# Filling the half-swapped input tile by copies on the chip instead of a second load from DRAM

## The reference, cut to what matters

```python
x = x + _L0_conv_ref(_gn(x), dw, pw, att, glob)   # stage 0
x = x + _L1_conv_ref(_gn(x), w_off, w_conv, b)    # stage 1

# stage 0: a 3x3 depthwise convolution, then three 32x32 channel mixes (softmax, 1x1, softmax)
# stage 1, a deformable 3x3 convolution:
off  = conv3x3(x, w_off)                # 64 channels: a row and a column offset for each pixel
rows = clip(off_row + r, 0, H - 1); cols = clip(off_col + c, 0, W - 1)
mapped = bilinear sample of x at (rows, cols)      # floor, ceil, four values, two blends
out  = conv3x3(mapped, w_conv) + b
```

## Time and profile before

| | us |
|---|---|
| median of 3 runs | 717.24 |
| lowest and highest run | 716.29, 727.23 |
| the profiled execution: its time | 718.9 |
| the profiled execution: its span | 717.1 |

### The profile page before, as it was taken

The page is one execution under the profiler, slowest core; times in us unless marked ns, Lnnn a source line. Parts: engine busy times, 40 slices in busy tenths (PEclk is TensorE's granted clock), DMA queues, the critical chain, the costliest instruction groups (busy, mean ns, idle before and its releaser), DMA issues.

```text
span 717.1 us, 10746 instructions
## 1 busy us (share of the span) xinstructions
PE 684.6 (95%) x3500; PEld 244.4 (34%) x3500; DVE 522.7 (73%) x1033; ACT 467.9 (65%) x812; POOL 478.1 (67%) x414
## 2 busy tenths in 40 slices
PE   4799979999999799999999999999999999999985
PEld 4333333333333233333333333333333333333322
DVE  3687988779956568677876589657984685578882
ACT  7587776686667365677556755576656775577870
POOL 5004867888597656866867765887658668788770
PEclk9999999999999899999999999999999999999998
DMA  8958926889557998799949896598947625477556
GB/s 142 187 111 144 143 57 158 179 178 196 126 141 165 189 213 204 171 209 189 203 112 233 173 209 152 138 236 171 225 112 177 154 66 139 114 170 178 123 118 147
DMA packets 140189, 115.64 MB, mean 161 GB/s; under 512 B 15168, under 2 KB 114016, under 8 KB 140128
## 3 DMA queue, kind: packets, MB, share of 16 engines
q1 hardware_dynamic: 116096, 103.12, 68.6%
q10 hardware_dynamic: 24032, 11.78, 9.2%
HBM read 31.59 MB, written 16.78 MB: 67 GB/s over the span
## 4 chain that ended last, share of the span: by engine, by line
PE 55%; SPq 5%; DVE 5%; ACT 3%; POOL 3%; issue 2%; DMA 1%; DVEq 0%; POOLq 0%; ACTq 0%
PE off_ps L794 27%; PE c_ps L683 24%; PE c_ps L694 2%; PE c_ps L698 2%; SPq L476 2%; SPq L395 1%; DVE other_row L1436 1%; SPq L427 1%; ACT other_row L988 1%; DMA x1b<-x1a 1%; ACT off_abs L1001 1%; DVE x1a L1421 1%; POOL row_diff L1213 1%; ACT down_ps L999 1%; POOL row_diff L1215 1%
## 5 line engine op out<-in xcount | busy, mean ns | idle before, releaser
L1436 DVE COPY_PREDICATED other_row<-down_ps,row_diff 128x768 f32<-128x768 int32 x128 | 124.7, 1028 | 124.2 <-ACT down_ps L999 124.0
L794 PE MATMUL off_ps<-x1a,wo 128*64 128x512 f32 x768 | 179.4, 601 | 4.3 <-DMA x1b<-x1a 3.7
L794 PE MATMUL off_ps<-x1b,wo 128*64 128x512 f32 x768 | 176.4, 592 | 0.0
L683 PE MATMUL c_ps<-xb,w 128*64 128x512 f32 x336 | 149.6, 593 | 2.2 <-DVE x1a L1421 1.6
L683 PE MATMUL c_ps<-mapb,w 128*64 128x512 f32 x336 | 150.8, 594 | 0.5 <-ACT bias L977 0.3
L685 PE MATMUL c_ps<-xa,w 128*64 128x512 f32 x336 | 149.6, 593 | 0.0
L988 ACT ACTIVATE other_row<-row_diff 128x768 f32<-128x768 f32 x128 | 100.7, 835 | 66.4 <-POOL row_diff L1215 43.8
L1230 POOL TENSOR_TENSOR other_row<-other_row,x_strips 128x512 f32<-128x512 f32 x48 | 57.2, 1191 | 119.1 <-DVE other_row L1448 119.0
L685 PE MATMUL c_ps<-mapa,w 128*64 128x512 f32 x294 | 131.7, 594 | 0.0
L999 ACT ACTIVATE down_ps<-off_ps,bias_o 128x512 f32<-128x512 f32 x64 | 42.0, 656 | 106.8 <-PE off_ps L794 99.4
L1231 POOL TENSOR_TENSOR other_col<-other_col,other_row 128x512 f32<-128x512 f32 x64 | 86.3, 1349 | 31.3 <-DVE other_row L1448 31.3
(11 more groups left out here) (135 smaller groups left out, 978.5 us busy)
## 6 DMA issues: line engine op xcount, KB each, us to landing
mapa<-mapped SPq DMA_DIRECT2D x224, 65.0 KB, 2.0
x1b<-x1a SPq DMA_DIRECT2D x28, 520.0 KB, 6.5
mapb<-mapa SPq DMA_DIRECT2D x28, 520.0 KB, 7.6
out_dram<-x1a SPq DMA_DIRECT2D x49, 256.0 KB, 4.7
xb<-in_x_dram SPq DMA_DIRECT2D x48, 256.0 KB, 9.9
xa<-in_x_dram ACTq DMA_DIRECT2D x40, 256.0 KB, 8.7
x_strips<-x1a SPq DMA_DIRECT2D x112, 81.2 KB, 2.5
x_strips<-x1a SPq DMA_DIRECT2D x112, 65.0 KB, 2.5
```

What stands on the lines that cost most here:

```text
L683: nc.tensor.matmul(bank[0:64, :], weights[:, kx, :], rows_b[:, of, kx:kx + W], start=(kx == 0), stop=(kx == 2))
L794: last = nc.tensor.matmul(off_ps[k % 2][64 * t:64 * t + 64, CH * n:CH * n + CH], wo[wpar][:, kx, side:side + 2 * C], rows[:, b:b + 7:2, kx ...
L1436: last = dve.copy_predicated(other_row[n][:, :, KR // 2 * odd:KR // 2 * odd + KR // 2, :], bass.AP(tensor=rows.tensor, offset=rows.offset ...
```

## The change

From image 1 on, `xb` is no longer loaded from DRAM. Once a half of `xa` has landed, SP copies it within SBUF to `xb`, whole rows with their pad columns, by two transfers of 64 partitions (one for each swapped half). Each takes runs of 16 x 130 floats, which is 520 KB a transfer, the size of an `x1b` copy. Where eight transfers of 256 KB were issued there are now four of 520 KB. Each copy waits for its half of `xa`, a wait that SP did not have. For images 3 to 7 the two halves are also put at different places of SP's list: the first half where the load stood, the second half behind the first half of the strips of the next image. ACT's wait ahead of `pad_x` counts two transfers a half instead of four.

```diff
...
@@ -448,15 +448,14 @@
                     sp.wait_ge(sem_, value)
                     sp.sem_inc(sp_step, 1)
 
-            def load_xb(i, half, loaded):
-
-                rows = x[i].rearrange("c (b r) w -> c b r w", r=4)
-                to = xb_of(i)
+            def copy_xb(i, half, copied):
+
+                to, rows = xb_of(i), xa_of(i)
                 b, e = half * HB, half * HB + HB
-                for q in range(4):
-                    first = b + 1 if q < 2 else b
-                    sp.dma_start(to[Q * q:Q * q + Q, first:first + HB, 1:W + 1], rows[:, b:e, (q + 2) % 4, :])\
-                      .then_inc(loaded[half], DMA)
+                for first, p, p_from in ((b + 1, 0, 2 * Q), (b, 2 * Q, 0)):
+                    sp.dma_start(to[p:p + 2 * Q, first:first + HB, :].rearrange("p b w -> p (b w)"),
+                                 rows[p_from:p_from + 2 * Q, b:e, :].rearrange("p b w -> p (b w)"))\
+                      .then_inc(copied[half], DMA)
 
             def copy_x1b(par, half):
                 n = NR // 4 * WP
@@ -514,7 +513,8 @@
                              conv_b.rearrange("(c o) -> c o", o=1)).then_inc(b_load, DMA)
             sp.wait_ge(cleared, 1)
             for half in range(2):
-                load_xb(1, half, ahead_xb_loaded)
+                sp.wait_ge(ahead_loaded[half], LOADS * DMA)
+                copy_xb(1, half, ahead_xb_copied)
 
             for strip in range(4):
                 sp.wait_ge(x1_ready, min(2 * strip + 3, 8))
@@ -525,7 +525,8 @@
                     sp.wait_ge(conv1_done, 8)
                     load_x(sp, 2, half, xa_loaded)
                 for half in range(2):
-                    load_xb(2, half, xb_loaded)
+                    sp.wait_ge(xa_loaded[half], xa_count(2))
+                    copy_xb(2, half, xb_copied)
 
             for i in range(NB):
                 prev, nxt, after = i >= 1, i + 1 < NB, i + 2 < NB
@@ -553,10 +554,9 @@
                     sp.wait_ge(mapa_moved[1], A_MOVES * DMA * i)
                     copy_mapb(1)
                 if after and prev:
-                    for half in range(2):
-
-                        sp.wait_ge(conv1_done, 8 * (i + 1) + (5 if half == 0 else 8))
-                        load_xb(i + 2, half, xb_loaded)
+                    sp.wait_ge(conv1_done, 8 * (i + 1) + 5)
+                    sp.wait_ge(xa_loaded[0], xa_count(i + 2))
+                    copy_xb(i + 2, 0, xb_copied)
                 if not prev:
                     sp.wait_ge(mapped_ready, 4)
                     sp.wait_ge(s_setup["dve"], 6)
@@ -568,8 +568,13 @@
                     sp.wait_ge(off_done, NK * i + 4)
                     copy_x1b((i + 1) % 3, 0)
                     sp.wait_ge(mapped_ready, NK * i + 4)
-                    for half in range(2 if i >= 2 else 1):
-                        move_strips(sp, i + 1, half)
+                    move_strips(sp, i + 1, 0)
+                    if prev and after:
+                        sp.wait_ge(conv1_done, 8 * (i + 1) + 8)
+                        sp.wait_ge(xa_loaded[1], xa_count(i + 2))
+                        copy_xb(i + 2, 1, xb_copied)
+                    if i >= 2:
+                        move_strips(sp, i + 1, 1)
                 if not nxt:
                     if i >= 2:
                         sp.wait_ge(out_ready, 8 * (i - 1))
@@ -619,7 +624,8 @@
                     for half in range(2):
                         load_x(sp, b, half, xa_loaded)
                     for half in range(2):
-                        load_xb(b, half, xb_loaded)
+                        wait_apart(xa_loaded[half], xa_count(v))
+                        copy_xb(b, half, xb_copied)
                     wait_apart(x1_pads, v + 1)
                     for half in range(2):
                         copy_x1b(0, half)
@@ -883,9 +889,9 @@
                 else:
                     for half in range(2):
                         if isinstance(i, int) and i == 1:
-                            act.wait_ge(ahead_xb_loaded[half], LOADS * DMA)
+                            act.wait_ge(ahead_xb_copied[half], COPIES * DMA)
                         else:
-                            act.wait_ge(xb_loaded[half], LOADS * DMA * (i - 1))
+                            act.wait_ge(xb_copied[half], COPIES * DMA * (i - 1))
                 rows_a, rows_b, mean = xa_of(i), xb_of(i), mean_x[par]
                 fill(rows_a[:, :, 0:WP:WP - 1], mean[:, :])
                 fill(rows_b[:, :, 0:WP:WP - 1], mean[:, :])
```

More of the change, by code:

```diff
@@ L251, in deformable_preact_kernel @@
         ahead_loaded = [sem(f"x_ahead_loaded{n}") for n in range(2)]
-        ahead_xb_loaded = [sem(f"x_ahead_xb_loaded{n}") for n in range(2)]
+        ahead_xb_copied = [sem(f"x_ahead_xb_copied{n}") for n in range(2)]
         x1b_written = sem("x1b_written")
         xb_written = sem("xb_written")
-        xb_loaded = [sem(f"xb_loaded{n}") for n in range(2)]
+        xb_copied = [sem(f"xb_copied{n}") for n in range(2)]
         x1b_copied = [sem(f"x1b_copied{n}") for n in range(2)]
```

## The result

| | median us | range | runs |
|---|---|---|---|
| before | 722.24 | 716.29 to 728.07 | 4 |
| with the change | 732.88 | 731.24 to 736.20 | 4 |

The four runs of before fall into two groups near 717 and 728, and the ratio, 1.023 with a 95% interval of 1.017 to 1.029, is that of the runs with the change to the two runs near 717. The profiled execution of the change took 733.4 us with a span of 731.6, against 718.9 and 717.1. The forecast was 722.5, with a range up to 728.5. The sign was right and the size was not. The time lies between the forecast and the rival that was slower by over 2% (736).

The account below looks back on a forecast made before the run. PE was taken to bound the kernel, busy 370 of 370 us from 252 to 622. Terms -3.2 + 5.6 + 3.0 = +5.4 on 718.9 gave 724.3, less 1.7 for the median 722.6, stated as 722.5; range 711.5 to 728.5.

Parts of the forecast that it names:

- the rival that was slower by over 2%: Late `xa` loads hold SP in image 4 and one later image, two 8 us gaps with low clock: 736 us, chance 0.1.
- The start, images 1 and 2: Eight loads become four copies, twice; new waits for `xa` fall into SP's 16.6 us of room, so nothing was counted.
- The price of a pair to the issues right behind it: In SP's list, a copy pair costs 1.3 us by itself and the issues behind it 3.3 us more.
- Image 3, a gain of 3.2 us: SP gains 1.5 us during image 1, PE's `x1b` gap in image 2 shrinks from 3.7 to 2.2: gain 3.2 us.
- Image 4, filled in image 2, a cost of 8.6 us: SP waits 4.4 us for late `xa`, `mapb` comes late: a new 5.6 us gap plus 3.0 us of low clock.
- Images 5 to 7, counted at nothing: SP 4.6 us later against room of 4.7, so 0 to 2 us; counted 0, PE's image 3 loss being room.
- The sum: Whole kernel: -3.2 + 5.6 + 3.0 = +5.4 us, given chance 0.45 and its own range of 719 to 727 us.
- The rule on turns between queues: DMA engines serve queues round-robin by packets, so ACT's late `xa` load gets its turn; the forecast set 21.1 us against it.
- the 10 us of an even share of the bytes: Rival for image 4: ACT's `xa` load gets half of 209 GB/s, no wait for `xa`; 714.7 us, chance 0.2.
- The 21.1 us of before: Landing time of image 4's last `xa` load, issued at 254.8 before the change; carried over to predict landing at 272.

Follow-up runs that it names:

- the one with the small pair: Against the kernel with image 4 loaded, the copy pair between the strips moved one block of 16 for images 3, 5, 6 and 7; 719.33 us, ratio 1.0015.
- the kernel with image 4 loaded: Against the change, image 4 alone had both halves of `xb` loaded from DRAM at the old place; 727.94 us, ratio 1.012.
- the first edit: Against the change, only images 1 and 2 were copied, both halves of images 3 to 7 loaded at the old place; 718.27 us, ratio 0.9994.
- Without the late load: Against the change, `xa` of image 4 was loaded behind chunks 1 and 3 of image 2, like the other images; 731.87 us, ratio 1.019.
- the kernel with only loads from image 4 on: Against the change, only images 1, 2 and the first half of image 3 were copied, all else loaded at the old place; 725.43 us, ratio 1.010.
- the one with copied first halves: Against the change, from image 3 on only first halves of 3, 5, 6 and 7 were copied, other halves loaded, all at the old place; 716.24 us, ratio 0.9967.
- a later load: Against the kernel with only loads from image 4 on, ACT's second half of `xa` came one chunk later in images 3 to 5; 713.98 us, ratio 0.9949.
- loads at the new place: Against the change, from image 3 on both halves were loaded from DRAM, the second still between the strips; 721.76 us, ratio 1.0045.

## Why the prediction was wrong

- **The start, images 1 and 2: right.** Copied or loaded is the same (0.9994).
- **The price of a pair to the issues right behind it: right.** 1.3 us and 3.3 more were taken, 1.2 and 3.0 were measured. For image 2 the forecast's terms without the wait for `xa` are 14.6 + 1.3 + 13.9 + 11.3 = 41.1 us from `x1b` to the store, and the list took 41.0.
- **Image 3, a gain of 3.2 us: wrong, it cost 2.1** (1.6 at `x1b`, 0.5 at `mapb`). The forecast had the `x1b` pair leave at 169.1 and take 14.6 us with its strips. It left 2.4 us later, at 171.46 (PE was 1.7 us late from the start), and took 15.9 (to 187.37). The first copy pair does not explain that, as it had landed by 168.2; the cause stays open. Behind the second pair the strips after the store took 11.4 us (10.6 before) and the second `mapa` 12.2 (11.8 before), where I had let SP's gain of 1.5 us carry through. In the six kernels that copy only the first half of image 3, and in the one with the small pair, the gain is there: PE waits 1.0 to 1.8 us for `x1b` and is then 4.0 to 5.1 us ahead of before. So the bytes of the second pair are what took it.
- **Image 4, filled in image 2, a cost of 8.6 us: wrong, it was 0.4.** SP was near the forecast, with the second `mapb` issue at 332.06 where it had 329.2. PE was not: it wanted `mapb` at 338.6 where the forecast had 331.6, since it was 3.8 us late and not 3.2 early, and it came when `mapb` had nearly landed (338.9). The 4.4 us wait for the second half of `xa` was not there: the load had landed at 274.8 when SP came at 275.1. The 12.3 us wait for its first half, which the forecast overlooked, was there and was covered by SP's wait for the pads of `x1a`.
- **Images 5 to 7, counted at nothing: this is the step that failed.** It is 10.7 of the 14.9 us. All of it falls in PE's image 4, 1.9 us as a wait for ACT and 8.8 at the `mapb` pair that stands in SP's list behind the pairs for image 5, filled in image 3. The forecast set SP's lateness at 4.6 us against a room of 4.7. In the kernel with image 4 loaded, the `mapb` pair of image 4 went out 9.3 us later than before with PE 1.7 later. So SP was 7.6 us late against PE and not 4.6: 1.1 at the start of the list, 5.0 in it, 1.5 behind it. PE lost 7.0 us there. At a landing of 7.4 us it would have waited 2.3. The landing, for which the forecast had no term here, took 3.4 more beside ACT's load, and the clock, at half for 3.4 us, cost the other 1.3. In the change, where the clock was at half for 6.8 us, it cost 2.9. "What PE lost in image 3 is room for the next images" held for no image, as PE lost 0.4 us there.
- **The sum.** Forecast -3.2, +8.6 and 0, measured +2.1, +0.4 and +10.7, and 1.7 us at the start that the runs of the first edit show not to be the change's. That the sign came out right was luck: the term that made it was not there, and the loss came from the one counted at nothing.
- **The rival slower than 2%** came nearest in time (736). It had two gaps of 8 us with low clock, where the trace has 5.3 and 5.85, but put them down to a late `xa` that spreads. Without the late load the time is the same (1.019 against 1.023, with intervals that overlap), so that is not the cause.
- **The rule on turns between queues.** The last of ACT's loads of `xa` for image 4 landed like this (count, KB, us to landing):

```profile
xa<-in_x_dram ACTq DMA_DIRECT2D x1, 256.0 KB, 16.9
```

That is 18.3 us for the half from its first issue, at 256.44, not the 10 us of an even share of the bytes. The 21.1 us of before, which the forecast carried over, are no measure of long rows: what SP had on the engines from 253 to 256 was its load of `xb`, 1054 packets with 0.52 MB, so rows of 512 bytes. By the page "DMA: Bandwidth & Descriptors" of the Trainium skill, section "Queues, rings and completion order", the turns go by packets, and this trace does not contradict that: ACT's rows are of 512 bytes and a row of the copies is of 8,320. Equal turns can then be unequal bytes. No run here separates this from other reasons.

What stays open: why the copied pair in SP's list costs up to 2.7 us more than four loads of the same bytes at the same place (41.0 against 38.3 us in image 2), so that the bytes are not the whole price, and why the kernel with only loads from image 4 on has a longer list in image 3 than the one with copied first halves (37.9 against 36.7).

## What to carry to other kernels

Here a copy within SBUF in place of a load from DRAM relieved neither the DMA engines, which moved 115.87 MB instead of 115.64, nor the list behind it, in which the strips behind a copied pair took longer than behind the loads. Count a transfer by what it holds up behind it, and in every stage that it is placed in. When a queue is only a few us ahead of need, look up what another queue issues just behind that point: being late past it costs the collision as well as the delay, and in this kernel 2.6 us of lateness made 7 us between two traces (9 between the medians). Before giving up a change, move the thing that it collides with, since a later load turned 725 into 714 us.

## What the runs showed of the hardware that I had not expected

- Two 520 KB copies within SBUF land 7.1 to 7.6 us after the first issue with nothing near them. With 1 MB of loads from another queue issued at the same moment it is 10.4 to 11.9 us.
- An issuing engine can be held up by the transfers of another engine's queue: SP's 32 strip issues took 27.6 us with ACT issuing the copies, 23.1 to 24.1 without them.
- Whether the clock falls behind a gap of PE does not go by its length alone. It fell to half for 3.4 us behind one of 2.2 us (loads at the new place) and did not behind one of 2.8 us in the same trace, nor behind one of 1.8 (first halves only). Around the gaps of 5 to 8 us it stood at half for 3.4 us (gaps of 5.6 and 5.7) or 6.8 (gaps of 5.85, 6.2 and 7.2).
